# A mixture-of-experts layer on eight cores: shared weights, gathers, scatters and router steps in another order

## The reference, cut to what matters

```python
xn = layernorm(x)
u  = xn @ B                                    # (.., 64)
hs = scan(h = sigmoid(A_diag) * h + u)         # over time
s  = hs @ C + xn @ D
r  = sigmoid(xn @ gate_w + gate_b)             # 16 experts
v, idx = top_k(r, 2);  v = v / sum(v)
mlp(x, wg, wu, wd) = (silu(x @ wg) * (x @ wu)) @ wd
f  = xn + mlp(xn, shared) + sum_k v_k * mlp(xn, expert[idx_k])
x  = x + s * silu(f)
```

## Time and profile before

| | us |
|---|---|
| runs before | 618.86, 621.00, 622.82; median 621.0 |
| profiled execution | 626.75 |
| its span on the slowest core (6) | 625.2 |
| spans of the others | 599.1 to 621.3 |
| PE busy | 478.8 (77%) |
| DVE busy | 211.0 (34%) |
| POOL busy | 185.7 (30%) |
| ACT busy | 156.4 (25%) |
| software DMA queue, share of 16 engines | 71.3% |
| hardware DMA queue | 19.8% |

### The profile page before, as it was taken

One profiled execution on the slowest core, in us unless ns is written; L12 is line 12 of the kernel. 1 busy time (PEld: TensorE's weight loads), 2 busy tenths in 40 slices (PEclk: granted clock), 3 DMA queues, 4 the chain that ended last, 5 costly groups with the idle time before them and its releaser, 6 DMA issues.

```text
span 625.2 us, 7885 instructions; the slowest of 8 cores (599.1 to 625.2 us)
## 1 busy us (share of the span) xinstructions
PE 478.8 (77%) x2814; PEld 263.6 (42%) x2840; DVE 211.0 (34%) x315; ACT 156.4 (25%) x240; POOL 185.7 (30%) x191
## 2 busy tenths in 40 slices
PE   0763954798968999996997997068758677978993
PEld 0662423354544645644454464035435333433441
DVE  4956600223212221220211121011112123778995
ACT  1760231232221313321232232013213111121221
POOL 2770470213312232240431243024102110433444
PEclk9999888789998888886888798579779899999997
DMA  8999769499999999999999999989999965798873
GB/s 225 333 331 164 120 118 176 82 170 183 222 156 191 179 186 210 154 197 193 149 209 161 181 188 175 172 188 166 194 205 153 189 181 204 211 305 287 312 281 151
DMA packets 29704, 122.70 MB, mean 196 GB/s; under 512 B 5276, under 2 KB 5660, under 8 KB 22880
## 3 DMA queue, kind: packets, MB, share of 16 engines
q0 software_dynamic: 17136, 81.15, 71.3%
q1 hardware_dynamic: 12528, 41.03, 19.8%
HBM read 150.86 MB, written 33.55 MB: 295 GB/s over the span
## 4 chain that ended last, share of the span: by engine, by line
PE 37%; DMA 36%; DVE 10%; issue 4%; DVEq 4%; POOL 3%; ACT 3%; POOLq 1%; SPq 1%; ACTq 0%
DMA xg<-xn_dram,gidx 24%; PE ps L384 12%; PE ps L388 12%; PE ps L752 10%; DMA ring<-y_dram 4%; DVEq L81 3%; DMA ring<-swu 3%; DMA y_dram<-ysb,pidx 3%; DVE ps L874 2%; PE ps L721 2%; DVE ps L871 2%; ACT ysb L877 2%; DMA x_sb<-x_in 2%; DVE sml L302 1%; POOL ring L278 1%
## 5 line engine op out<-in xcount | busy, mean ns | idle before, releaser
L752 PE MATMUL ps<-ring,xgT 128*128 128x512 bf16 (+1 forms) x379 | 104.6, 421 | 31.3 <-ACT ysb L763 15.4
L405 DVE TENSOR_TENSOR xgT<-silu,ps 128x320 bf16<-128x320 f32 x64 | 31.3, 488 | 223.8 <-ACT silu L398 223.8
L384 PE MATMUL ps<-xgT,ring 128*128 128x320 bf16 x512 | 93.2, 332 | 0.9 <-ACT xgT L729 0.9
L388 PE MATMUL ps<-xgT,ring 128*128 128x320 bf16 x512 | 90.1, 325 | 0.0
L398 ACT ACTIVATE silu<-ps 128x320 f32<-128x320 f32 (+1 forms) x80 | 37.6, 469 | 177.7 <-PE ps L388 175.3
L752 PEld LDWEIGHTS ps<-ring,xgT 128*128 128x128 bf16 (+1 forms) x384 | 36.7, 109 | 95.7 <-issue 77.9
L721 PE MATMUL ps<-cbf,xg 128*128 128x128 bf16 x336 | 30.0, 237 | 54.7 <-DMA xg<-xn_dram,gidx 49.8
L388 PEld LDWEIGHTS ps<-xgT,ring 128*128 128x128 bf16 x512 | 54.2, 106 | 25.9
L384 PEld LDWEIGHTS ps<-xgT,ring 128*128 128x128 bf16 x512 | 52.2, 107 | 27.8 <-issue 6.2
L765 DVE COPY ysb<-ps 128x512 f32<-128x512 f32 (+1 forms) x48 | 33.2, 691 | 85.7 <-PE ps L752 70.2
L851 PE MATMUL ps<-ring,xnT 128*128 128x512 bf16 x252 | 61.1, 384 | 0.2
(11 more groups left out here) (141 smaller groups left out, 439.4 us busy)
## 6 DMA issues: line engine op xcount, KB each, us to landing
ring<-ewg POOLq DMA_DIRECT2D x16, 1024.0 KB, 20.5
ring<-ewu POOLq DMA_DIRECT2D x16, 1024.0 KB, 20.6
ring<-ewd POOLq DMA_DIRECT2D x16, 1024.0 KB, 17.8
ring<-y_dram SPq DMA_DIRECT2D x32, 512.0 KB, 6.0
x_sb<-x_in SPq DMA_DIRECT2D x16, 512.0 KB, 13.3
out<-ysb SPq DMA_DIRECT2D x16, 512.0 KB, 3.1
ring<-x_in SPq DMA_DIRECT2D x6, 512.0 KB, 19.8
ring<-dmat POOLq DMA_DIRECT2D x2, 1024.0 KB
```

What stands on the lines that cost most here:

```text
L384: PE.op(lambda e, c=c: e.matmul(bank(p)[:, 0:n], slot_gu(m, c, ic), rhs(c), start=(c == 0), stop=(c == 7)))
L388: f = lambda e, c=c: e.matmul(bank(2 + p)[:, 0:n], slot_gu(m + 1, c, ic), rhs(c), start=(c == 0), stop=(c == 7))
L405: T_MUL[key] = V.sig(lambda e: e.tensor_tensor(dst, silu[:, p * 512:p * 512 + n], bank(2 + p)[:, 0:n], ALU.mult))
L752: f = lambda q, k=k, h=h, dst=dst: q.matmul(dst, inter(e, k, o, n), slot_d(m, k, h), start=(k == 0), stop=(k == 3))
```

## The change

- swg and swu are asked for on POOL after the norm of the tenth own tile (`i == 11`); the other two weights follow when the store of own tile 12 has landed.
- Shared group 0 is put ahead of the rank and count matmuls in PE's queue; four groups instead of three precede the inv matmuls, and 6 instead of 5 the experts. The products of groups 4 and 5 are made by DVE instead of POOL.
- The router's step from packed value to column and row is shorter (`st_col` is gone; column = value >> 7, row = value & 127). V is built by 32 `tensor_scalar` operations of 128 columns instead of two `tensor_tensor` of 2048.
- Five gathers, not four, are issued ahead of the three weights before expert 0.
- In each expert the gathers are issued ahead of the loads, and the scatters ahead of the load after down. From expert 14 on no load is issued after gate-up: the two dmat weights follow the scatters of experts 14 and 15.
- The count of extra rounds is read on PE, ACT, DVE and POOL at expert 2 instead of after the last expert.
- In the tail the first products of tiles 0 and 1 precede PE's wait for the dmat weights.

```diff
--- before.py
+++ after.py
@@ -30,7 +30,8 @@
 NXR = 12
-NEARLY = 5
+NEARLY = 6
+NPOOL = 4
 PAD = 16384
@@ -415,10 +416,15 @@
             p = T_GU[key][1]
+            if g >= NPOOL:
+                gate_mul(key, 512, interS[:, ic * T_OWN + tb * 512:ic * T_OWN + (tb + 1) * 512])
+                return
             T_UPC[g] = A.sig(lambda e: e.activation(upc[p], bank(2 + p), AF.Copy))
...
         def sh_mul(g):
+            if g >= NPOOL:
+                return
             tb, ic = divmod(g, 4)
@@ -439,10 +445,12 @@
                 xn_store(t, i)
+                if i == 11:
+                    load_w(2)
             j = i - AHEAD
...
                 logits(ORDER[j])
-        load_w(4)
+        load_w(2, T_ST[12])
 
@@ -553,55 +561,50 @@
 
+
+        e_, r_ = sm(4), sm(5)
+
         def st_int():
             V.drain()
-            V.op(lambda e: e.tensor_scalar(smi[:, SN:2 * SN], smi[:, 0:SN], 12, 63,
-                                           ALU.logical_shift_right, ALU.bitwise_and))
-            V.op(lambda e: e.tensor_scalar(smi[:, 2 * SN:3 * SN], smi[:, 0:SN], 18, None,
+            V.op(lambda e: e.tensor_scalar(smi[:, SN:2 * SN], smi[:, 0:SN], 12, None,
                                            ALU.logical_shift_right))
-            V.op(lambda e: e.tensor_scalar(smi[:, 3 * SN:4 * SN], smi[:, 0:SN], 4095, None,
+            V.op(lambda e: e.tensor_scalar(smi[:, 2 * SN:3 * SN], smi[:, 0:SN], 4095, None,
                                            ALU.bitwise_and))
             V.drain()
-            V.op(lambda e: e.tensor_copy(sml[:, 4 * SN:7 * SN], smi[:, SN:4 * SN]))
-            V.drain()
+            V.op(lambda e: e.tensor_copy(sml[:, 4 * SN:6 * SN], smi[:, SN:3 * SN]))
+            V.drain()
+            V.op(lambda e: e.scalar_tensor_tensor(sm(7), e_, float(CAP), r_, ALU.mult, ALU.add))
+            V.op(lambda e: e.tensor_scalar(sm(8), r_, float(CAP), 12800.0, ALU.is_ge, ALU.mult))
+            V.drain()
+            V.op(lambda e: e.tensor_tensor(smi[:, 0:SN], sm(7), sm(8), ALU.add))
+            V.drain()
+            V.op(lambda e: e.tensor_scalar(smi[:, SN:2 * SN], smi[:, 0:SN], 7, None,
+                                           ALU.logical_shift_right))
+            V.op(lambda e: e.tensor_scalar(smi[:, 2 * SN:3 * SN], smi[:, 0:SN], 127, None,
+                                           ALU.bitwise_and))
+            V.drain()
+            V.op(lambda e: e.tensor_copy(sml[:, 9 * SN:11 * SN], smi[:, SN:3 * SN]))
         steps.append(st_int)
 
-        q_, o_, r_ = sm(4), sm(5), sm(6)
-
-        def st_col():
-            V.op(lambda e: e.tensor_scalar(sm(7), r_, 128.0, None, ALU.is_ge))
-            V.op(lambda e: e.tensor_scalar(sm(8), r_, 256.0, None, ALU.is_ge))
-            V.op(lambda e: e.tensor_scalar(sm(9), r_, float(CAP), None, ALU.is_ge))
-            V.drain()
-            V.op(lambda e: e.tensor_tensor(sm(7), sm(7), sm(8), ALU.add))
-            V.op(lambda e: e.tensor_tensor(sm(8), sm(8), o_, ALU.mult))
-            V.drain()
-            V.op(lambda e: e.scalar_tensor_tensor(sm(10), sm(7), -128.0, r_, ALU.mult, ALU.add))
-            V.op(lambda e: e.scalar_tensor_tensor(sm(7), q_, 5.0, sm(7), ALU.mult, ALU.add))
-            V.op(lambda e: e.tensor_tensor(sm(11), o_, sm(8), ALU.subtract))
-            V.drain()
-            V.op(lambda e: e.scalar_tensor_tensor(sm(10), sm(8), 64.0, sm(10), ALU.mult, ALU.add))
-            V.op(lambda e: e.scalar_tensor_tensor(sm(7), sm(11), 3.0, sm(7), ALU.mult, ALU.add))
-            V.drain()
-            V.op(lambda e: e.scalar_tensor_tensor(sm(7), sm(9), 100.0, sm(7), ALU.mult, ALU.add))
-        steps.append(st_col)
         def st_u():
...
                 v3(r_E, SN), cst(C_I40, NCOL)[:, None, :].broadcast_to((128, SN, NCOL)),
-                over(sm(7), NCOL), ALU.is_equal))
+                over(sm(9), NCOL), ALU.is_equal))
             G.wait(R["E"])
...
                 v3(r_U, SN)[:, :, NCOL:2 * NCOL], v3(r_E, SN), over(cst(C_TK, SN), NCOL), ALU.mult))
-            for h in range(2):
-                R["V"] = V.sig(lambda e, h=h: e.tensor_tensor(
-                    v3(r_V[:, h * 2048:(h + 1) * 2048], 16),
-                    cst(C_IO, 128)[:, None, :].broadcast_to((128, 16, 128)),
-                    over(sm(10)[:, h * 16:(h + 1) * 16], 128), ALU.is_equal))
+            for i in range(SN):
+                f = lambda e, i=i: e.tensor_scalar(r_V[:, i * 128:(i + 1) * 128], cst(C_IO, 128),
+                                                   sm(10)[:, i:i + 1], None, ALU.is_equal)
+                if i < SN - 1:
+                    V.op(f)
+                else:
+                    R["V"] = V.sig(f)
         steps.append(st_u)
@@ -666,9 +669,11 @@
 
+        sh_gu(0)
         until("cnt")
         until("E")
-        for g in range(3):
+        sh_mul(0)
+        for g in range(1, NPOOL):
             sh_gu(g)
@@ -780,22 +785,25 @@
         T_SA = V.sig(lambda e: e.reciprocal(a_t[:, 3:4], a_t[:, 2:3]))
-        for j in range(4):
+        for j in range(5):
             gather(j)
...
         FREE_DB[4] = R["invr"]
-        for g in range(3, NEARLY):
+        for g in range(NPOOL, NEARLY):
             sh_gu(g)
-            sh_mul(g)
-        A.wait(T_MUL["s", NEARLY - 1], T_MUL["s", NEARLY - 2])
-        G.wait(T_MUL["s", NEARLY - 1], T_MUL["s", NEARLY - 2])
+        FREE_INT[-1] = T_MUL["s", NPOOL - 1]
         for p in parts(0):
             transpose_tile(0, *p)
-        for j in (4, 5, 6):
+        for j in (5, 6):
             gather(j)
...
             FREE_Y[b] = R["inv"]
+
+        n_extra = {}
+
+        def count(e):
+            return e.value_load(xcnt[0:1, E:E + 1]).with_bounds(min_val=0, max_val=E * XTILES)
 
@@ -833,6 +841,10 @@
         def tail_front(t):
+            tail_p1(t)
+            tail_p2(t)
+
+        def tail_p1(t):
             b = 4 * (t % 2)
@@ -843,6 +855,9 @@
                         PE.op(f)
+
+        def tail_p2(t):
+            b = 4 * (t % 2)
             PE.wait(T_H.get(t - 2))
@@ -905,15 +920,21 @@
                 st_w()
-                V.wait(*[T_MUL["s", g] for g in (NEARLY - 2, NEARLY - 1)])
+                V.wait(*[T_MUL["s", g] for g in range(NPOOL)])
+                G.wait(T_MUL["s", NPOOL - 1])
                 T_CS = [V.sig(lambda e: e.memset(csb[DS:128, :], 0.0)),
...
                 recur(e - 1)
-            load_w(len(free_places))
+            if e == 2:
+                for Q in (PE, A, V, G):
+                    Q.wait(R["tot"])
+                    Q.op(lambda e, Q=Q: n_extra.__setitem__(id(Q), count(e)))
             for p in nxt:
...
                     gather(p[0] + NXG)
+            if e < E - 2:
+                load_w(len(free_places))
             PE.wait(T_W[m + 2], *[T_MUL[(e, ic)] for ic in range(4)])
@@ -923,9 +944,9 @@
             free_w(m + 2, k)
-            load_w(len(free_places))
             for y in ys[0:2] if e % 2 == 0 else ys:
                 scatter(y[0])
+            load_w(1 if e == E - 2 else len(free_places))
 
@@ -937,21 +958,15 @@
 
-        def count(e):
-            return e.value_load(xcnt[0:1, E:E + 1]).with_bounds(min_val=0, max_val=E * XTILES)
-
         LASTV, LASTA = (s_v, s_v.n), (s_a, s_a.n)
...
         LASTG = list(y_last.values())
-        for Q in (PE, A, V, G):
-            Q.wait(R["tot"])
-
         def after(e, *toks):
...
         def pe_extra(e):
-            n = count(e)
+            n = n_extra[id(PE)]
             with e.If(n > 0):
...
@@ -1113,11 +1126,16 @@
             T_YF[t] = y_load(t)
-        PE.wait(T_DV, T_DA, *T_CS, T_W[M_SD], T_W[M_D0], T_W[M_D1], *[T_MUL[("s", g)] for g in range(16)])
-        tail_front(0)
+        PE.wait(T_DV, T_DA, T_W[M_SD], *[T_MUL[("s", g)] for g in range(16)])
+        tail_p1(0)
+        tail_p1(1)
+        PE.wait(*T_CS, T_W[M_D0], T_W[M_D1])
+        tail_p2(0)
         tail_sum(0)
         for t in range(NT):
-            if t + 1 < NT:
+            if t == 0:
+                tail_p2(1)
+            elif t + 1 < NT:
                 tail_front(t + 1)
@@ -1153,7 +1171,7 @@
     consts[:, C_W:C_W + E] = (E - ex)[None, :]
-    consts[:, C_PK:C_PK + E] = (4096 * (ex // 2 + 64 * (ex % 2)))[None, :]
+    consts[:, C_PK:C_PK + E] = (4096 * ex)[None, :]
     consts[:, C_GB:C_GB + E] = f["L0_ffn_gate_b"][None, :]
```

More of the change, by code:

```diff
@@ L982, in act_extra @@
         def act_extra(e):
-            n = count(e)
+            n = n_extra[id(A)]
             with e.If(n > 0):
@@ L991, in dve_extra @@
         def dve_extra(e):
-            n = count(e)
+            n = n_extra[id(V)]
             with e.If(n > 0):
@@ L995, in dve_extra @@
                 e.drain()
-                e.scalar_tensor_tensor(sm(7), q_, 2.0, o_, ALU.mult, ALU.add)
-                e.drain()
-                e.scalar_tensor_tensor(sm(7), sm(7), float(T_OWN), r_, ALU.mult, ALU.add)
+                e.scalar_tensor_tensor(sm(7), e_, float(T_OWN), r_, ALU.mult, ALU.add)
                 e.drain()
@@ L1055, in pool_extra @@
```

(2 more changed lines are left out.)

## The result

The changed kernel takes 637.1 us (median of 4 runs, 631.9 to 643.4) against 620.7 us (618.9 to 622.8, 4 runs) for the kernel before on the same chip: ratio 1.024, 95% interval 1.016 to 1.031. It is slower by 16 us (whether by more than 2% the interval leaves open); the forecast was 612, range 599 to 624.

A forecast was written before the change was run, and what follows sets the result against it. DMA work plus DMA holes was taken to bound the kernel from first gather to last expert. 8.9 - 7.7 - 3 - 7 - 1 + 0.5 = -9.3 us took the 621.0 median to 612, range 599 to 624.

The forecast's parts named there:

- (a): Prologue: early shared weights and group 0 ahead of the rank hold up the router; +8.9 us, range +2 to +13.
- My condition for failure: Prediction fails if late x tiles stretch the norm, or PE's lower clock becomes the bound of the experts.
- Equal shares: Prologue DMA queues: weights and x tiles with stores share the engines equally, swu landing at 63.4 us; 63 taken.
- The V build inside (a): Router's V on DVE: 4.6 us of steps, 2.15 beside U, 1.3 for POOL's products of groups 0 and 1.
- (b): Before expert 0: five gathers ahead of weights close the DMA hole at 110 us; -7.7 us, range -5 to -9.
- (c): Every expert: gathers ahead of loads remove gather waits, worth only small DMA holes; -3 us, range 0 to -5.
- (d): Expert ends: scatters no longer wait behind swd, last dmat weights follow scatters; -7 us, range 0 to -15.
- (f): Tail: first shared products moved ahead give nothing, last dmat weight may push y loads; +0.5 us, range 0 to +7.
- rival 3: Tail: expert 14's scatter wait unchanged, deferred dmat weight lands beside the y loads; +8.2 us, 629; chance 0.11.
- (e): Final chain: count read at expert 2 under cover of DMA; -1 us, or 0 if the drain awaits the scatter.
- (g): Before expert 0: group 5 early, products of groups 4 and 5 on DVE; nothing more within 31 us of DMA.
- rivals, 2: Prologue eats the gain: +13 to the first gather, scatter reordering only -3; sum -0.7 us, 620; chance 0.22.

The follow-up runs named there:

- self_wait: Changed kernel with POOL's drain behind the nmr product replaced by a wait on that product's own semaphore: 623.0 us, ratio 1.008.
- v_slow: Kernel before with only V built by 32 one-input steps instead of two two-input operations: 616.1 us, ratio 1.000.
- queue_dmat: Kernel before with five gathers first, gathers and scatters ahead of loads, swd and dmat loads not put off: 608.9 us, ratio 0.989.
- done_memset: Changed kernel with POOL's drain ahead of the y loads replaced by a one-column memset: 638.6 us, no ratio given.
- late_two_dmat: late_two with the swd and dmat loads not put off: 602.4 us, ratio 0.976.
- early_only: Kernel before with only swg and swu asked for amid the norm, the other two weights after it: 632.9 us, ratio 1.030.
- late_two: Changed kernel without early request and the two drains, V in two operations, group 0 behind the rank, two groups ahead of inv: 600.5 us, ratio 0.984.

## Why the prediction was wrong, point by point

**Part (a) failed first.** It put the early request at +8.9 us; the first gather came 18.8 us late. The step that failed is the one that moved two loads into the norm and counted only the queues they enter. It didn't ask what POOL does next: the drain behind the next nmr product. It stands for 20.2 us and costs 11.1 (self_wait), since without it the stores hold up the router. My condition for failure spoke of late x tiles; the norm did stretch, though the tiles were there.

Without the stall the number would have stood: self_wait's first gather at 88.2 against the 88.7 forecast. But that was luck, for the reason was wrong. swu landed at 54.3, not 63, and the rank waited for DVE and a store, not for group 0. "Equal shares" was the false step there. On core 2 of self_wait, queues from 41 to 48 us (packets, MB, share of 16 engines):

```profile
q0 software_dynamic: 132, 0.95, 90.0%
q1 hardware_dynamic: 129, 0.24, 10.0%
```

The two queues got equal numbers of packets, and the weights' are four times as large (7.2 against 1.9 KB) and took nine tenths of the time. The Trainium skill states this in "DMA: Bandwidth & Descriptors", section "Queues, rings and completion order": an engine takes turns between its queues packet by packet. From 41 to 48 us the trace agrees, with 132 against 129 (134 against 137, 137 against 138 and 135 against 133 on cores 0, 4 and 6); I had read shares where I should have read packets.

The V build inside (a) was put at 4.6 + 2.15 + 1.3 = 8.05 us and measured 12.5. Two terms were mis-sized. The steps follow each other at 0.196 us (the last 26 take 5.17 us, from 88.43 us on), so 32 undisturbed ones are 6.3 us, not 4.6; the 0.165 and 5.3 us in the expectation of v_slow are too low. And U and all four products fell into it, not U and two. The mechanism was right. The steps ahead of V gave some of it back: from the rank to V's start it is 8.05 us, before 10.05, so 2.0 us less where 0.6 had been forecast. By the rule of the Trainium skill that the prediction weighed ("SBUF — State Buffer", section "SBUF: two separate sides") a whole operation blocks the other engine, and the trace agrees for these one-input steps too: 2.36 us beside U, 1.28 to 1.31 beside each product.

**Parts (b) and (c)** were right in kind. The hole closed, PE's waits went from gathers to weights, and the order alone shortens the experts by 8.8 us (queue_dmat). The prediction gave (b), (c) and (d) 17.7 us together, of which (d)'s share includes swd put behind the scatters; about half came. How the rest is shared among the three the runs don't tell, since they were only run together; but the wait of (d) can be read.

**Parts (d) and (f)** together: -7 and +0.5 were given. (d) took 6.8 us off the scatter that expert 14's eviction waits for, because swd is asked for behind it now. swd is (at 467.61 us, POOL), and the scatter took longer all the same. The chain has it as

```profile
460.03 28.00 DMA y_dram<-ysb,pidx
```

where the earlier trace rows had 18.43 us. It is 22.4 to 29.5 us on the eight cores, in v_slow 15.4 to 19.2, and PE's wait for the eviction behind it is 5.5 to 12.6 us, in v_slow 2.4 to 6.2. So the step that failed in (d) is "swd stands behind it: 6.8 us less". The weights take longer to land too (ewg 29.5 us in the median, before 20.5), so more stands ahead of each transfer than before; that this is the reason isn't shown. On the medians expert 15's last up matmuls begin at 496.8 us, 10.5 later than in v_slow, with a first gather 18.8 later: what the experts gain, they gain in spite of this wait.

The way to the first sum is 6.9 us longer, at the upper end of the range for (f), and at most 3.8 us of it come back in the experts. This is rival 3's mechanism, weights that land beside the y loads; what (d) is worth in time isn't shown. The sentence "free by 1 us" failed: it compared the landing with the product's old date and left out that the drain ahead of the y loads waits for this load (12.7 us, before 4.75), and that without the drain the load and the y loads share the engines (done_memset).

**Part (e)**: the drain grew, so the microsecond for the count can't be seen. **Part (g)** wasn't run apart.

In sum: predicted +8.9 to the first gather, measured +18.8; -17.7 in the experts, measured -7.8; +0.5 less 1 behind them, measured +6.9, and 0.9 gained in the rest. So (a) was 9.9 us off, the experts 9.9 and the way behind them 7.4. No one of them makes the sign: with (a) as forecast the stages would still add up to +7.1, and self_wait, without the stall, is at 1.008. Nor does the stall alone leave the range: 612 + 9.9 is 622. Of the rivals, 2 and 3 were both partly true, and none had the stall.

## What to carry to other kernels

Before a DMA is moved on a queue, read on from its new place: a drain on the issuing engine may turn it into a wait for its landing. Where only the order of that engine's own results is meant, wait on the last result's semaphore. An early request is no gift either: it takes engine time by packets from small stores, so ask which of both somebody waits for. Run the parts of a bundled change apart: here the queue order with the loads left in place gains 1.1% (queue_dmat); late_two_dmat, which takes the rest of the change as well, but without the early request and the two drains, with V in two operations and two groups ahead of inv, gains 2.4%.

## What the runs showed of the hardware that I had not expected

- GpSimd's drain ends when the DMAs that GpSimd issued have landed: 19.0 to 20.7 us with two 1 MB loads under way (after and early_only, all cores), in the changed kernel 0.2 to 0.3 us behind the second landing, gone with a wait on the product's semaphore in its place; in the tail 9.7 to 12.7 us with one load, 4.0 to 5.6 in the kernel before, whose loads are all asked for ahead of the last scatters.
- Two DMA queues with work share an engine by packets: 132 and 129 packets in 7 us, 90% and 10% of the time. A 256 KB store, asked for from 34 us on, lands after 9 to 11 us where no weights are asked for before 42 us (late_two), and after up to 26 where they are asked for at 33 (self_wait).
- In the same place 32 short one-input steps on DVE lose 6.2 us beside five GpSimd operations, and two long two-input ones 3.1 us; there two GpSimd products take 3.3 us instead of 1.26.
